# A factorization-machine tower on one core: the order of ScalarE's and VectorE's one-hot units in the first two chunks

## The chip, the core and the metric

One of the eight cores of a Trainium2 chip runs the whole program. The metric is the device time of one execution in microseconds (us), from which a median of several runs is taken. Engines are named TensorE (PE in the profile, its weight loads PEld), VectorE (DVE), ScalarE (ACT), GpSimd (POOL) and SyncE (SP, which only issues DMAs here).

## What is computed

For each of 2048 rows the kernel looks up 40 embeddings of 32 numbers, forms the 780 pairwise bilinear products and puts them, with 16 dense values, through a small MLP:

```
e = stack([tbl_f[ids[:, f]] for f in range(40)], axis=1)      # 2048 x 40 x 32
z = einsum('bke,kef,bkf->bk', e[:, I], W, e[:, J])            # 780 pairs (I < J)
h = concatenate([z, dense_ctx], axis=1)                       # 2048 x 796
h = maximum(h @ W_top1 + b_top1, 0)                           # 512
h = maximum(h @ W_top2 + b_top2, 0)                           # 256
y = h @ W_top3                                                # 1
```

## The kernel before

The batch is worked through in 4 chunks of 512 rows. The 40 fields stand in 10 groups of four; one group, transposed, fills a tile eT of 128 partitions (4 fields of 32) by 512. The pairs are put into 50 quads per chunk (`plan_quads`), numbered 0 to 199 over all chunks. For each quad TensorE does a `transform` (line 670, matmuls of line 680: weights times eT into the banks tps, in two halves), VectorE multiplies each half with another eT tile (line 660, into prods, which has three slots), and TensorE does a `reduce` (lines 692 to 705, into the bank zps). The rows of z of eight quads fill one tile; then ScalarE's `drain_z` (line 500) copies zps to zs, and the next `reduce` with slot 0 waits for it.

**How groups get into eT.** Sixteen fields have tables of 1000 rows: groups 0 to 3, the hot ones. Groups 4 to 9 are gathered by GpSimd (line 484) and transposed by VectorE (line 612), one quad before they are first needed. A hot group is looked up by matmuls: the table lies in SBUF in eight units of 128 rows, and for each unit u of a hot group h a one-hot tile `hot` of 128 x 2048 is made, which TensorE multiplies with three bf16 parts of the table (`look_up`, line 715, matmuls of line 733), 12 matmuls for a unit. All eight units of a group add up in the bank mlp_ps, and ScalarE's `drain_hot` (line 536, activation of line 540) copies it to eT. The next group's first look-up waits for that drain (`bank_free`). In the text (h, u) is unit u of hot group h; h runs over all chunks: 0 to 3 belong to chunk 0, 4 to 7 to chunk 1, and so on.

**Who makes a unit.** `by_scalar` (line 188) says it. VectorE makes one with a single comparison (line 605). ScalarE needs two activations (lines 531 and 534: absolute distance, then a relu). The tile `hot` has four slots, so unit number n waits until TensorE has used unit n - 4 (`hot_used`). The ids come by a DMA per group into one of three slots (`load_ids`, line 403).

**When.** `SIDES` says in which quad TensorE looks a unit up: groups 2 and 3 in quads 0 to 3, four units a quad; the 32 units of groups 4 to 7 from quad 7 on, in three of four quads. `MAKES` says in which quad's place in the queues a unit is made; for groups 4 to 7 that is two quads ahead on ScalarE and three on VectorE (line 213). VectorE makes the units of a quad behind that quad's two products (lines 662 to 664). `IDS_AT` places the loads of ids among SP's other issues, two quads behind the last unit that used the slot; `MIXED_AT` places the copies that build mixed tiles (`mix`, line 422), whose products are in the third and later quads after the pair's second group is first used.

Everything runs on TensorE in cycles (`CYCLES`): quad 0 alone, then two quads together. In a cycle TensorE does transform(at), reduce(at - 1), the look-ups of at, transform(at + 1), reduce(at), the look-ups of at + 1. ScalarE's queue for a cycle (lines 569 to 582) holds, in this order: the drains of MLP tiles, the z drain if a tile of eight quads ends, the drain of a hot group if its last unit is looked up in this cycle, and last the units to be made. Three units of groups 2 and 3 are written out ahead of the loop (lines 564, 566, 568), between the roundings of the table's parts (`round_part`); the matching remainders are VectorE's (`rest`, line 591), between its own first units (lines 625 to 640).

In chunks 1 to 3 the MLP of the chunk before (line 753) runs beside the quads; the last chunk's runs at the end.

Of the kernel before, what the change touches and what calls it, by code (L numbers as in the profile page):

```python
# [104 lines left out]
def mlp_out(layer, m):  # L105
    return sum(outs for _, outs in LAYERS[:layer]) + m
# [8 lines left out]
HOT_COUNT = (4, 4, 4, 4)  # L115
HOTS = [(t, g) for t in range(CHUNKS) for g in range(HOT_COUNT[t])]
GATHERED = [(t, g) for t in range(CHUNKS) for g in range(HOT_COUNT[t], GROUPS)]

UNITS, PARTS_OF = 8, 3
HOT_SLOTS = 4  # L120
# [67 lines left out]
def by_scalar(h, u):  # L188


    t, g = HOTS[h]
    return [g > 1 and u % 4 == 3, ((h - HOT_COUNT[0]) * UNITS + u) % 3 > 0, u % 2 == 1][min(t, 2)]


def made_until(h, u, scalar):

    return sum(by_scalar(h_, u_) == scalar for h_ in range(len(HOTS)) for u_ in range(UNITS) if (h_, u_) <= (h, u))
# [5 lines left out]
MAKES = {at: [] for at in range(TOTAL)}  # L203
MAKES[0] = [(2, u) for u in range(HOT_SLOTS, UNITS)]
for unit in range(UNITS):
    MAKES[1 + unit // HOT_SLOTS].append((3, unit))
for side_at, items in SIDES.items():
    for item in items:
        if item[0] == "hot" and HOTS[item[1]][0] > 1:
            MAKES[side_at - MADE_AHEAD].append(item[1:])  # L210
        elif item[0] == "hot" and HOTS[item[1]][0] == 1:

            MAKES[side_at - (2 if by_scalar(*item[1:]) else 3)].append(item[1:])


def steps_of(at):
    return [item for item in SIDES[at] if item[0] == "mlp"]
# [65 lines left out]
def wait(engine, semaphore, count):  # L283
    if count > 0:
        engine.wait_ge(semaphore, count)
# [11 lines left out]
def build(nc, ids, bases, table, hot_ids, hot_table, dense, wt, w1, b1, w2, b2, w3, out):  # L297
    ctx = ExitStack()
    with ctx:
# [77 lines left out]
        def slot_free(engine, k):  # L377

            if k >= ET_SLOTS:
                t, g = divmod(k - ET_SLOTS, GROUPS)  # L380
                engine.wait_ge(multiplied, 2 * (t * QUADS + last_quad(g) + 1))

        def slot_of(t, g):
            return (t * GROUPS + g) % ET_SLOTS
# [104 lines left out]
        @block.scalar  # L489
        def _(act):  # L490
            def split_at(g, part):

                return SPLITS.index((g, part)) + 1

            def drain_z(t, kt):
                if t == 0 and kt == 0:

                    act.wait_ge(remainder, len(SPLITS))
                act.wait_ge(reduced, t * QUADS + min((kt + 1) * PER_KT, QUADS))
                act.activation(zs[:, t % 2, kt, :], zps[:, :], ACT.Copy).then_inc(z_drained, 1)  # L500

            def drain_mlp(t, banks, layer, m):
                out_tile = mlp_out(layer, m)
                act.wait_ge(mlp_filled, t * MLP_OUTS + out_tile + 1)
                if layer < 2:
                    dst, bias = [(h1s, b1s), (h2s, b2s)][layer]
                    act.activation(dst[:, m, :], banks[out_tile], ACT.Relu,  # L507
                                   bias=bias[:, m:m + 1]).then_inc(mlp_drained, 1)
                else:
                    wait(act, y_stored, t * 16)  # L510

                    act.activation(y_s[:, :], banks[out_tile][:, 0:CHUNK // Q],
                                   ACT.Copy).then_inc(mlp_drained, 1)
                    act.wait_ge(mlp_drained, t * MLP_OUTS + MLP_OUTS)
                    act.dma_start(out[0:1, t * CHUNK:(t + 1) * CHUNK].rearrange("o (q b) -> (o q) b", q=Q),
                                  y_s[0:PART:EMB, :]).then_inc(y_stored, 16)

            def round_part(g, part):
                if part == 0:
                    act.wait_ge(hot_table_loaded[g], 16)  # L520
                else:
                    act.wait_ge(remainder, split_at(g, part - 1))
                act.activation(part_of[g][part], raw_parts[g], ACT.Copy).then_inc(rounded, 1)  # L523

            def make_unit(h, u):

                if u == [by_scalar(h, u_) for u_ in range(UNITS)].index(True):
                    act.wait_ge(hot_ids_loaded[h % IDS_SLOTS], 16 * (h // IDS_SLOTS + 1))
                act.wait_ge(hot_used, h * UNITS + u - HOT_SLOTS + 1)
                columns = hot[:, (h * UNITS + u) % HOT_SLOTS].rearrange("p q c -> p (q c)")  # L530
                act.activation(columns, ids16[:, h % IDS_SLOTS].rearrange("p q c -> p (q c)"), ACT.Abs,  # L531
                               bias=minus_code[:, u:u + 1]).then_inc(distances, 1)
                act.wait_ge(distances, made_until(h, u, True))
                act.activation(columns, columns, ACT.Relu, scale=-1.0, bias=ones[:, 0:1]).then_inc(hot_made_act, 1)  # L534

            def drain_hot(h):
                t, g = HOTS[h]
                act.wait_ge(hot_used, (h + 1) * UNITS)
                slot_free(act, t * GROUPS + g)
                act.activation(eT[:, slot_of(t, g), :], mlp_ps[:, :], ACT.Copy).then_inc(hot_drained, 1)  # L540

            def drain_sums(at):

                if at >= 0 and (at % QUADS == QUADS - 1 or at % QUADS % PER_KT == PER_KT - 1):
                    drain_z(at // QUADS, at % QUADS // PER_KT)

            def drain_tiles(steps):
                for _, t, layer, m, k in steps:
                    if k == LAYERS[layer][0] - 1:
                        drain_mlp(t, between_banks, layer, m)  # L550

            round_part(0, 0)
            round_part(0, 1)
            act.wait_ge(code_built, 1)
            act.activation(minus_code[:, :], code[:, :], ACT.Copy, scale=-1.0).then_inc(codes_turned, 1)
            round_part(1, 0)
            round_part(1, 1)
            round_part(2, 0)
            drain_hot(0)
            drain_hot(1)  # L560
            round_part(2, 1)
            act.wait_ge(codes_turned, 1)
            act.wait_ge(consts_built, 2 + Q)
            make_unit(2, 3)
            round_part(3, 0)
            make_unit(2, 7)
            round_part(3, 1)
            make_unit(3, 3)
            for cycle in CYCLES:
                at = cycle[0]  # L570
                if at == QUADS + 1:
                    act.wait_ge(mlp_loaded, 16 * 5)
                drain_tiles(steps_of(at))
                drain_sums(at - 1)
                if len(cycle) == 2:
                    drain_sums(at)
                for kind, *step in [item for quad in cycle for item in SIDES[quad]]:
                    if kind == "hot" and step[1] == UNITS - 1:
                        drain_hot(step[0])
                for unit in [unit for quad in cycle for unit in MAKES[quad]]:  # L580
                    if by_scalar(*unit) and unit not in ((2, 3), (2, 7), (3, 3)):
                        make_unit(*unit)
            drain_z(CHUNKS - 1, KT - 1)
            for layer, (_, outs) in enumerate(LAYERS):
                for m in range(outs):
                    drain_mlp(CHUNKS - 1, last_banks, layer, m)
            act.wait_ge(y_stored, 16 * CHUNKS)

        @block.vector
        def _(dve):  # L590
            def rest(g, part):

                dve.wait_ge(rounded, SPLITS.index((g, part)) + 1)
                if part == 1:
                    dve.wait_ge(remainder, SPLITS.index((g, 0)) + 1)
                dst = raw_parts[g] if part == 0 else part_of[g][2]
                dve.tensor_tensor(dst, raw_parts[g], part_of[g][part], ALU.subtract).then_inc(remainder, 1)

            def make_unit(h, u):
                if h == 0 and u == 0:  # L600
                    dve.wait_ge(code_built, 1)
                if u == [by_scalar(h, u_) for u_ in range(UNITS)].index(False):
                    dve.wait_ge(hot_ids_loaded[h % IDS_SLOTS], 16 * (h // IDS_SLOTS + 1))
                wait(dve, hot_used, h * UNITS + u - HOT_SLOTS + 1)
                dve.tensor_scalar(hot[:, (h * UNITS + u) % HOT_SLOTS], ids16[:, h % IDS_SLOTS],  # L605
                                  code[:, u:u + 1], None, ALU.is_equal).then_inc(hot_made_dve, 1)
# [27 lines left out]
            for u in range(UNITS):  # L634
                make_unit(1, u)
            rest(2, 0)
            for u in range(HOT_SLOTS - 1):
                make_unit(2, u)
            rest(2, 1)
            rest(3, 0)  # L640
# [2 lines left out]
            for at in range(TOTAL):  # L643
                t, n = divmod(at, QUADS)
# [221 lines left out]
```

## Time and profile before

| | us |
|---|---|
| runs | 693.02, 693.56, 695.09; median 693.56 |
| profiled execution | 690.86 |
| its span, first to last instruction | 689.1 |
| mean granted TensorE clock | 0.993 |
| TensorE busy | 653.5 (95%) |
| VectorE busy | 537.8 (78%) |
| ScalarE busy | 277.2 (40%) |
| GpSimd busy | 374.5 (54%) |

"Busy" is the time in which an engine had an instruction in work; TensorE's matmuls are pipelined and their ends are modelled, so that a short wait can hide in a longer matmul. A releaser (`<-`) is the instruction whose end let another start; `[1.99 <-ACT hot L534]` behind a line means that the engine stood idle 1.99 us until ScalarE's write of `hot` in line 534. `x12` is the number of instructions merged into a line. The granted clock is 1.00 at 2.4 GHz and 0.50 at 1.2 GHz. The chain that ended last is followed backwards from the last instruction, at each step to what released it. A slice of the page is 17.2 us.

### The profile page before, as it was taken

How to read it: one execution, taken by the hardware profiler on the slowest of the kernel's cores; microseconds unless marked ns; L12 is line 12 of the kernel's file. 1: busy time of each engine (PE TensorE's matmuls, PEld its weight loads, DVE VectorE, ACT ScalarE, POOL GpSimd, SP SyncE). 2: the span in 40 equal slices, each digit the busy share in tenths (PEclk: the TensorE clock that was granted, in tenths of full speed). 3: DMA queues.
4: the chain of work that ended last, by engine and by line, in shares of the span. 5: the costliest groups of instructions: out<-in, count | busy, mean ns of one | idle time of the engine just before them, and what ended most of it. 6: DMA issues, size and time to landing. Idle time of an engine off the chain costs nothing.

```text
span 689.1 us, 11819 instructions
## 1 busy us (share of the span) xinstructions
PE 653.5 (95%) x5120; PEld 203.5 (30%) x5120; DVE 537.8 (78%) x515; ACT 277.2 (40%) x196; POOL 374.5 (54%) x391
## 2 busy tenths in 40 slices
PE   3779889888999999999999999999999999999998
PEld 1222223222233333233333323333332323223233
DVE  6776789889879898879768989797767878789910
ACT  3634855876636455647034545655210000100002
POOL 5774576666566566565556556565564666560000
PEclk9989999999999999999999999999999999999999
DMA  7392111203320303012311202001202201101000
GB/s 250 103 377 86 48 52 41 58 13 87 79 68 11 87 12 88 10 43 58 87 23 46 87 11 57 10 14 46 66 13 55 55 13 20 48 12 48 1 1 0
DMA packets 26707, 39.40 MB, mean 57 GB/s; under 512 B 9168, under 2 KB 15456, under 8 KB 26528
## 3 DMA queue, kind: packets, MB, share of 16 engines
q1 hardware_dynamic: 14336, 32.33, 14.5%
q0 software_dynamic: 12288, 6.32, 6.1%
q8 instruction: 40, 0.66, 0.4%
q14 instruction: 11, 0.09, 0.0%
q10 hardware_dynamic: 32, 0.01, 0.0%
HBM read 22.88 MB, written 0.01 MB: 33 GB/s over the span
## 4 chain that ended last, share of the span: by engine, by line
PE 89%; ACT 5%; DMA 2%; DVE 2%; SPq 1%; issue 1%; DVEq 0%; ACTq 0%
PE tps L680 31%; PE zps L702 27%; PE mlp_ps L753 15%; PE mlp_ps L733 12%; PE tps L753 4%; ACT hot L534 2%; ACT hot L531 2%; DVE prods L660 2%; DMA eT<-eT 1%; DMA ids<-in_hot_ids 1%; SPq L432 1%; PE zps L689 0%; ACT zs L500 0%; ACT eT L540 0%; PE mlp_ps L758 0%
## 5 line engine op out<-in xcount | busy, mean ns | idle before, releaser
L660 DVE TENSOR_TENSOR prods<-tps,eT 128x1024 f32<-128x1024 f32 x400 | 468.6, 1217 | 109.9 <-PE tps L680 106.4
L484 POOL DMA_INDIRECT rows<-in_table,idx x384 | 373.8, 974 | 245.9 <-DVE prods L660 136.9
L680 PE MATMUL tps<-eT,weights 32*128 32x512 f32 x1600 | 242.9, 643 | 8.3 <-ACT eT L540 6.2
L702 PE MATMUL zps<-prods,select 128*32 128x512 f32 x1600 | 207.4, 607 | 0.8 <-DVE prods L660 0.3
L531 ACT ACTIVATE hot<-ids,minus_code 128x2048 bf16<-128x2048 int16 x57 | 113.7, 1994 | 41.1 <-PE mlp_ps L733 41.0
L733 PE MATMUL mlp_ps<-hot,parts 128*32 128x512 bf16 x1536 | 106.0, 390 | 23.6 <-ACT hot L534 10.8
L534 ACT ACTIVATE hot<-hot,ones 128x2048 bf16<-128x2048 bf16 x57 | 114.1, 2002 | 1.9
L680 PEld LDWEIGHTS tps<-eT,weights 32*128 32x128 f32 x1600 | 70.7, 183 | 135.9 <-DVE prods L660 72.1
L753 PE MATMUL mlp_ps<-zs,w1s 128*128 128x512 f32 x182 | 85.6, 608 | 0.0
L702 PEld LDWEIGHTS zps<-prods,select 128*32 128x32 f32 x1600 | 35.5, 108 | 150.7 <-DVE prods L660 88.5
L500 ACT ACTIVATE zs<-zps 128x512 f32<-128x512 f32 x28 | 16.7, 597 | 150.7 <-PE zps L702 144.5
L733 PEld LDWEIGHTS mlp_ps<-hot,parts 128*32 128x32 bf16 x1536 | 43.9, 99 | 110.3 <-issue 61.6
L605 DVE TENSOR_SCALAR hot<-ids,code 128x2048 bf16<-128x2048 int16 x71 | 52.1, 756 | 0.5 <-DMA ids<-in_hot_ids 0.4
L507 ACT ACTIVATE h1s<-mlp_ps,b1s 128x512 f32<-128x512 f32 x13 | 8.9, 687 | 101.4 <-PE mlp_ps L753 101.4
L753 PEld LDWEIGHTS mlp_ps<-zs,w1s 128*128 128x128 f32 x182 | 32.4, 189 | 51.2 <-issue 45.9
L540 ACT ACTIVATE eT<-mlp_ps 128x512 f32<-128x512 f32 x16 | 9.5, 596 | 53.2 <-PE mlp_ps L733 53.1
L753 PE MATMUL mlp_ps<-h1s,w2s 128*128 128x512 f32 x48 | 22.7, 610 | 0.0
L507 ACT ACTIVATE h2s<-mlp_ps,b2s 128x512 f32<-128x512 f32 x6 | 4.1, 687 | 41.5 <-PE mlp_ps L753 41.5
L753 PE MATMUL tps<-zs,w1s 128*128 128x512 f32 x42 | 18.6, 594 | 0.0
L612 DVE STREAM_TRANSPOSE eT<-rows 128x512 f32<-128x512 f32 x24 | 16.8, 702 | 0.0
L753 PEld LDWEIGHTS mlp_ps<-h1s,w2s 128*128 128x128 f32 x48 | 8.5, 189 | 13.7 <-issue 12.2
L523 ACT ACTIVATE parts<-zs 128x1024 bf16<-128x1024 f32 x8 | 8.3, 1050 | 9.8 <-DMA zs<-in_hot_table 4.9
(28 smaller groups left out, 44.6 us busy)
## 6 DMA issues: line engine op xcount, KB each, us to landing
ids<-in_hot_ids SPq DMA_DIRECT2D x16, 512.0 KB, 4.9
eT<-eT SPq DMA_DIRECT2D x40, 192.0 KB
rows<-in_table,idx POOLq DMA_INDIRECT x384
eT<-eT SPq DMA_DIRECT2D x40, 128.0 KB
eT<-eT SPq DMA_DIRECT2D x40, 64.0 KB
zs<-in_hot_table SPq DMA_DIRECT2D x4, 512.0 KB, 8.5
w1s<-in_w SPq DMA_DIRECT2D x1, 1792.0 KB
weights<-in_wt SPq DMA_DIRECT2D x1, 960.0 KB, 8.9
```

What stands on the lines that cost most here:

```text
L484: pool.indirect_dma_start(rows[:, k % ROW_SLOTS, m * EMB:(m + 1) * EMB], None, table, bass.IndirectOffsetOnAxis(ap=idx[:, g, t, m:m + 1], ...
L500: act.activation(zs[:, t % 2, kt, :], zps[:, :], ACT.Copy).then_inc(z_drained, 1)
L507: act.activation(dst[:, m, :], banks[out_tile], ACT.Relu, bias=bias[:, m:m + 1]).then_inc(mlp_drained, 1)
L531: act.activation(columns, ids16[:, h % IDS_SLOTS].rearrange("p q c -> p (q c)"), ACT.Abs, bias=minus_code[:, u:u + 1]).then_inc(distances, 1)
L534: act.activation(columns, columns, ACT.Relu, scale=-1.0, bias=ones[:, 0:1]).then_inc(hot_made_act, 1)
L605: dve.tensor_scalar(hot[:, (h * UNITS + u) % HOT_SLOTS], ids16[:, h % IDS_SLOTS], code[:, u:u + 1], None, ALU.is_equal).then_inc(hot_made_ ...
L612: dve.transpose(eT[:, slot_of(t, g), :], rows[:, k % ROW_SLOTS, :]).then_inc(transposed, 1)
L660: dve.tensor_tensor(prods[:, at % PROD_SLOTS, 2 * half:2 * half + 2, :], tps[:, (2 * at + half) % PAIR_BANKS, :, :], tiles, ALU.mult).then ...
L680: last = pe.matmul(tps[:, (2 * at + half) % PAIR_BANKS, bank, :], weights[part, n, :], eT[part, slot_of(t, g), :], start=True, stop=True)
L702: last = pe.matmul(zps[EMB * r:EMB * (r + 1), :], select[:, off:off + EMB], prods[:, at % PROD_SLOTS, bank, :], start=kt < KT - 1 and slot ...
L733: last = pe.matmul(mlp_ps[EMB * q:EMB * (q + 1), :], part_of[g][part][:, col:col + EMB], hot[:, at % HOT_SLOTS, q, :], start=u == 0 and pa ...
L753: last = pe.matmul(banks[out_tile], [w1s, w2s][layer][:, k, m * PART:(m + 1) * PART], [zs[:, t % 2, k, :], h1s[:, k % M1, :]][layer], star ...
```

## The change

It gives one unit of group 2 and one of group 3 to ScalarE, (2,5) and (3,5), instead of two each. (2,5) stands between the rounding of parts (3,0) and (3,1), (3,5) in the loop at the cycle of quads 3 and 4; VectorE makes the others, four of group 2 ahead of the loop instead of three. In ScalarE's loop the units of groups 2 to 7 (made for chunks 0 and 1) stand ahead of the cycle's drains; those of later chunks stay behind them. VectorE's units of groups 4 to 7 are made four quads ahead of their use instead of three. Two loads of ids follow in SP's order: that of group 6 from quad 4 to 5, that of group 8 from quad 26 to 25.

```
-    return [g > 1 and u % 4 == 3, ((h - HOT_COUNT[0]) * UNITS + u) % 3 > 0, u % 2 == 1][min(t, 2)]
+    return [g > 1 and u == 5, ((h - HOT_COUNT[0]) * UNITS + u) % 3 > 0, u % 2 == 1][min(t, 2)]
...
 for unit in range(UNITS):
-    MAKES[1 + unit // HOT_SLOTS].append((3, unit))
+    MAKES[3 if by_scalar(3, unit) else 1 + unit // HOT_SLOTS].append((3, unit))
...
-            MAKES[side_at - (2 if by_scalar(*item[1:]) else 3)].append(item[1:])
+            MAKES[side_at - (2 if by_scalar(*item[1:]) else 4)].append(item[1:])
...
             act.wait_ge(consts_built, 2 + Q)
-            make_unit(2, 3)
             round_part(3, 0)
-            make_unit(2, 7)
+            make_unit(2, 5)
             round_part(3, 1)
-            make_unit(3, 3)
             for cycle in CYCLES:
...
+                units = [unit for quad in cycle for unit in MAKES[quad] if by_scalar(*unit) and unit != (2, 5)]
+                for unit in units:
+                    if HOTS[unit[0]][0] < 2:
+                        make_unit(*unit)
                 drain_tiles(steps_of(at))
                 drain_sums(at - 1)
...
-                for unit in [unit for quad in cycle for unit in MAKES[quad]]:
-                    if by_scalar(*unit) and unit not in ((2, 3), (2, 7), (3, 3)):
+                for unit in units:
+                    if HOTS[unit[0]][0] > 1:
                         make_unit(*unit)
...
             rest(2, 0)
-            for u in range(HOT_SLOTS - 1):
+            for u in range(HOT_SLOTS):
                 make_unit(2, u)
             rest(2, 1)
```

## Rows read from the trace of the kernel before

**Rows 1.** The page: busy time and share by engine, then slices of TensorE and its clock.

```profile
PE 653.5 (95%) x5120; PEld 203.5 (30%) x5120; DVE 537.8 (78%) x515; ACT 277.2 (40%) x196; POOL 374.5 (54%) x391
...
PE   3779889888999999999999999999999999999998
...
PEclk9989999999999999999999999999999999999999
```

**Rows 2.** Waits, 66 to 200 us: engine, line <- releaser: us, times, longest.

```profile
PE mlp_ps L733 <- ACT hot L534: 10.4, 5, 2.6
```

**Rows 3.** TensorE in order of time, 66 to 205 us: start, us, operation, idle before.

```profile
75.71 0.90 PE L733 MATMUL mlp_ps<-hot,parts 128*32 128x512 bf16 x12 [1.99 <-ACT hot L534]
...
101.09 0.83 PE L733 MATMUL mlp_ps<-hot,parts 128*32 128x512 bf16 x12 [2.65 <-ACT hot L534]
...
114.66 1.50 PE L680 MATMUL tps<-eT,weights 32*128 32x512 f32 x8
...
124.73 0.83 PE L733 MATMUL mlp_ps<-hot,parts 128*32 128x512 bf16 x12 [1.93 <-ACT hot L534]
...
198.07 3.70 PE L753 MATMUL mlp_ps<-zs,w1s 128*128 128x512 f32 x8
```

**Rows 4.** ScalarE in order of time, 120 to 131 us.

```profile
120.16 0.60 ACT L500 ACTIVATE zs<-zps 128x512 f32<-128x512 f32 x1 [7.43 <-PE zps L702]
120.65 1.99 ACT L531 ACTIVATE hot<-ids,minus_code 128x2048 bf16<-128x2048 int16 x1
...
124.59 1.99 ACT L531 ACTIVATE hot<-ids,minus_code 128x2048 bf16<-128x2048 int16 x1
...
130.91 0.60 ACT L540 ACTIVATE eT<-mlp_ps 128x512 f32<-128x512 f32 x1 [2.30 <-PE mlp_ps L733]
```

**Rows 5.** TensorE in order of time, 36 to 57 us.

```profile
36.28 4.02 PE L733 MATMUL mlp_ps<-hot,parts 128*32 128x512 bf16 x48
44.98 1.51 PE L680 MATMUL tps<-eT,weights 32*128 32x512 f32 x8 [4.68 <-ACT eT L540]
...
48.12 3.22 PE L733 MATMUL mlp_ps<-hot,parts 128*32 128x512 bf16 x48
51.27 1.14 PE L680 MATMUL tps<-eT,weights 32*128 32x512 f32 x8
...
53.22 3.09 PE L733 MATMUL mlp_ps<-hot,parts 128*32 128x512 bf16 x48
```

**Rows 6.** ScalarE in order of time, 40 to 57 us.

```profile
40.40 2.00 ACT L531 ACTIVATE hot<-ids,minus_code 128x2048 bf16<-128x2048 int16 x1 [4.55 <-PE mlp_ps L733]
...
44.34 0.58 ACT L540 ACTIVATE eT<-mlp_ps 128x512 f32<-128x512 f32 x1
...
56.37 0.60 ACT L540 ACTIVATE eT<-mlp_ps 128x512 f32<-128x512 f32 x1 [0.94 <-PE mlp_ps L733]
```

**Rows 7.** VectorE in order of time, 60 to 117 us.

```profile
60.54 0.75 DVE L605 TENSOR_SCALAR hot<-ids,code 128x2048 bf16<-128x2048 int16 x1
...
64.68 2.36 DVE L660 TENSOR_TENSOR prods<-tps,eT 128x1024 f32<-128x1024 f32 x2 [1.12 <-DMA eT<-eT]
...
111.26 4.85 DVE L660 TENSOR_TENSOR prods<-tps,eT 128x1024 f32<-128x1024 f32 x4
116.03 0.70 DVE L612 STREAM_TRANSPOSE eT<-rows 128x512 f32<-128x512 f32 x1
```

**Rows 8.** TensorE in stretches: length, busy (matmuls), granted clock, DMA share, GB/s.

```profile
46.00:48.00 2.00, 2.00 (x12) 0.50 0.96 389
78.00:80.00 2.00, 2.00 (x12) 0.56 0.11 16
98.00:100.00 2.00, 0.45 (x7) 1.00 0.06 11
```

**Rows 9.** The chain that ended last, 55 to 66 us: start, us, what.

```profile
60.20 4.46 DMA eT<-eT
```

**Rows 10.** GpSimd in order of time, 104 to 109 us.

```profile
104.77 0.95 POOL L484 DMA_INDIRECT rows<-in_table,idx  x1 [0.30 <-issue]
```

## The prediction

> **What bounds the kernel now.** I read the page first: TensorE is busy 653.5 us of the 689.1 us span, and the slices of its line show where it isn't: almost all digits below 9 lie in the first eleven of 40 slices, that is in the start and in chunk 0; from chunk 1 on TensorE is full [rows 1]. The change touches only what is made for chunks 0 and 1, all of it made while chunk 0 runs. So a microsecond that TensorE saves before 198 us comes off the end whole, and nothing can be gained later.
>
> Next, the waits of 66 to 200 us: TensorE stood five times, 10.4 us together, for a unit that ScalarE had not finished [rows 2]. TensorE's own order of time shows the five: 1.99 us before the matmuls at 75.71, 2.65 before 101.09, 1.93 before 124.73, and twice more 1.93 (at 148.39 and 171.97) [rows 3]; added up 10.43. They come every eight quads, which is the rhythm of the z drains. ScalarE's order of time shows why: at 120.16 it drains z after 7.43 us of idling, only then starts the unit at 120.65, and needs two activations for it (until the next unit starts at 124.59: 3.94 us a unit); the stalled matmuls start at 124.73 [rows 3, 4]. The unit didn't depend on the drain; it stood behind it in ScalarE's queue. The five are (4,2), (5,0), (5,6), (6,4) and (7,2), used in quads 9, 17, 25, 33 and 41.
>
> At the start the same happens the other way round. Unit (3,3) waits until group 2 has been used up, starts at 40.40, and the drain of group 2 (eT at 44.34) stands behind it, although its bank was full at 36.28 + 4.02 = 40.30. TensorE stands idle 4.68 us, until 44.98 [rows 5, 6].
>
> **Part 1: group 2's and 3's units.** ScalarE gives up (2,3), (2,7), (3,3), (3,7) and takes (2,5), (3,5). VectorE gets two units more, at 0.75 us each [rows 7].
> - (2,3) is now a fourth VectorE unit ahead of rest(2,1). That delays the third part of group 2's first look-up by 0.75 us; the cover is the wait for the first mixed tiles, which ends with the same DMA as before, with over 1 us to spare. Cost nothing; if the cover is gone, 0.75 us.
> - (3,3) no longer stands ahead of drain_hot(2): the drain starts at 40.4 and transform(2) at 44.98 - 3.93 = 41.05. VectorE makes (3,3) behind the products of quad 1, before TensorE's look-ups of quad 2. **Gain 3.9**; the lower bound is 3.9 - 0.75, if VectorE's fourth unit is in the way.
> - The clock. In 46 to 48 us TensorE was granted 0.50, its level of 1.2 GHz, behind the gap of 4.68 us [rows 5, 8]. The stretch from transform(2) to transform(3) took 51.27 - 44.98 = 6.29 us; the same work of quad 3 took from 51.27 to 53.22 + 3.09 = 56.31, 5.04 us, at full clock [rows 5]. Without the gap I take full clock: **gain 1.2**. Bounds: 0 (the level falls all the same) and 1.25.
> - Look-ups of quad 3: (3,5) needs (3,1) used, which is so in the middle of quad 2's look-ups; it then has a transform and a reduce as cover. (3,6), (3,7) go to VectorE behind the products of quad 2, 1.5 us. drain_hot(3), before at 56.37 [rows 6], comes 5.1 us earlier; nothing more.
> - Mixed tiles of pair 1: SP issues them on drain_hot(3); the last copy took 4.46 us from 60.20 and VectorE waited 1.12 us for it [rows 7, 9]. The load of group 6's ids, which SP issued just ahead of these copies, now stands behind them (its quad goes from 4 to 5), so the copies don't share the DMA engines with 512 KB. And unit (4,0), 0.75 us between products of quads 4 and 5, is made while VectorE waits for transform(4). Together up to 1.12 + 0.75 = 1.87; (4,3), now ahead of quad 8's products, takes back some 0.3. **Gain 1.5**, bounds 0 and 1.87.
>
> **Part 2: units ahead of the drains.** (4,2) can start right behind (4,1), as its slot is long free; the others have the idle time ahead of the z drain: 7.43 us before 120.16 for 3.94 us of work [rows 4]. Each of the five stalls goes. **Gain 1.99 + 2.65 + 3 x 1.93 = 10.4.** With the first of them goes a half-speed stretch: granted clock 0.56 in 78 to 80 us, right behind the stall that ended at 75.71 [rows 3, 8]. **Gain 1.1**, sized like the other one. Bounds 0 and 1.25.
>
> What is late next? A unit that is still being made when a drain falls due. The narrowest place is between the z drain of 120.16 and the drain of group 5 at 130.91: 10.75 us apart now, 8.8 without the stall of 1.93. In it ScalarE has the z drain (0.49, from 120.16 to 120.65), (6,0) and now (6,1) too: 0.49 + 2 x 3.94 = 8.4 [rows 3, 4]. It fits with 0.4 us to spare, and behind it TensorE has a transform and a reduce, some 2 us, before it needs the bank. At drain 6 and at the z drains more is left. Cost nothing; without that cover up to 3.9 each.
>
> **Part 3: VectorE's units one quad sooner.** The same instructions, moved by one quad. They leave the place where TensorE runs a quad without look-ups, and enter the one ahead of it. Nothing was waiting for these units, but a product behind one is 0.75 later and those two quads on are no later. Cost and gain between -0.3 and +0.4 in each of nine four-quad stretches; I take 0.
>
> Does VectorE carry the faster pace? Four products take 116.03 - 111.26 = 4.77 us, so 1.19 each [rows 7]. From 75.71 to 198.07 [rows 3] lie 41 quads: 82 x 1.19 = 97.6, 10 units 7.5, five transposes 3.5: 108.6 of 122.4 us. Without the later four stalls (8.44) 114 are left, 5 more than VectorE needs. GpSimd: group 7's last gather was issued at 104.77, its transpose began at 116.03 [rows 7, 10]; with the stalls gone that lead loses 2 to 3 us of 11.
>
> **Sum.** 3.9 + 1.2 + 1.5 + 10.4 + 1.1 = 18.1 us. The profiled execution took 690.86 us (span 689.1), so it would come to 672.8. It was 2.7 us below the median of the three runs, 693.56; against that median I forecast **675.4 us**.
>
> **A rule for the other side.** ScalarE's drain of group 2 stood 3.93 us behind a unit it had nothing to do with [rows 6]. The Trainium skill, page "TensorE: Matmul & The Clock Gate", section "Architectural detail: the array is 16× 32×32, not 1× 128×128", says that ScalarE and VectorE take their queues strictly in order, only TensorE may reorder. By that rule a unit put ahead of a drain is as able to hold TensorE up as a drain ahead of a unit; the trace agrees in both directions.
>
> **Clock, rule and row.** The stall that ended at 101.09 is longer than that at 75.71, yet the clock stayed at 1.00 in 98 to 100 [rows 3, 8]. So the first slow stretch need not be the work of the stall. The same page, section "What's actually happening", says that the throttled state is the default and that activity lifts it. By it the fuller TensorE should keep 2.4 GHz, with the sum as it stands; by the row at 98 to 100 alone, 2.3 us of the sum would be open.
>
> **Rivals.**
> - *The slow stretches stay or move.* For it: the row at 98 to 100. Against: both stood right behind a gap. 18.1 - 2.3 = 15.8 gained, **677.7 us**. Chance 0.14.
> - *VectorE becomes the bound.* With 5 us of slack over 41 quads and products buffered only three deep, TensorE waits in small pieces where it stood in large ones. If half of the 8.44 comes back: **679.6 us**. For it: VectorE is on the chain already between the stalls. Against: it waits for TensorE in each stretch. Chance 0.15.
> - *More than forecast.* Behind each quad without look-ups a transform takes 1.50 us, as at 114.66, instead of 1.14 as at 51.27 [rows 3, 5]: it waits for products. Nine such places; if the earlier units remove them all, 3.2 to 3.6 more, **671.8 us**. Chance 0.07.
> - *Slower: drains held by units.* Eight drains in chunk 0 get a unit directly ahead of them (z0 to z4, groups 3, 5, 6). Each could be late by 3.94 less some 1.3 us that TensorE has in hand: 8 x 2.6 = 21.1, against 18.1 gained: 3 us slower, **696.6 us**. It decides from 2.3 us on at each drain, that is where a unit starts under 0.4 us before its drain falls due. Against it: the idle time of 7.43 ahead of the z drain [rows 4]. Chance 0.02.
> - *The order changes nothing*: the units wait for hot slots that come free only at the drains, and the stalls stay. Then only part 1 acts: 6.6 gained, **687.0 us**. Against: (5,6) needs (5,2), used five quads earlier. Chance 0.03; in 0.02 of it the gap at 40 to 45 is refilled by VectorE's units as well, and no difference is left that can be measured.
>
> The forecast keeps 0.59. The range 671.5 to 681.0 takes in the first three rivals and the bounds of the terms. A measurement of this kernel can tell about 0.3%, 2.1 us, from no change. Faster by more: 0.96, all cases but two; within: 0.02, the end of the last one; slower by more: 0.02, the drains held.
>
> **What would show it.** TensorE's waits for ScalarE's units between 60 and 200 us nearly gone; transform(2) at about 41; no gap of over 4 us at 40 to 45; granted clock 1.00 at 46 to 48 and around 70; the z drains behind two activations of a unit, at about 64, 86, 108, 130 and 151; the first MLP matmuls at about 180 instead of 198.07, and the same distance from there to the end. It is wrong if TensorE waits for eT or zs behind a unit, if VectorE has no waits left in chunk 0, or if the MLP start moves by less than 12.

## The result, and the profile after

The changed kernel takes 674.61 us, median of 4 runs (673.34 to 675.00), against 693.29 for the kernel before in 4 runs (691.10 to 695.09). The ratio is 0.9729 with a 95% interval from 0.9697 to 0.9760: 2.7% faster. The forecast was 675.4. The profiled execution took 673.34 us with a span of 671.5, so 17.6 us of span are gone, where the working had 18.1. Of the runs below, ten fell on chips where the kernel before itself took 814 to 848 us, with TensorE pausing where no other engine held it; those are set only against the kernel before as it ran beside them, and read for who waited for whom.

The page of the changed kernel: TensorE has lost 4 us of busy time, which goes with fewer stretches at the lower clock and shorter matmuls that no longer hold a wait, and the digits below 9 have gone from its slices behind the start [rows 1].

```profile
span 671.5 us, 11817 instructions
...
PE 649.5 (97%) x5120; PEld 204.6 (30%) x5120; DVE 538.2 (80%) x517; ACT 269.7 (40%) x192; POOL 373.3 (56%) x391
...
PE   3789999999999999999999999999999999999998
...
PEclk9989999999999999999999999999999999999999
```

The waits from 60 to 200 us. TensorE's own five waits for ScalarE's units, 10.4 us [rows 2], have no row any more; what is left is 0.6 us in its weight loads. VectorE still waits 12.2 us for TensorE, in 21 pieces.

```profile
DVE prods L665 <- PE tps L685: 12.2, 21, 1.9
...
PEld mlp_ps L738 <- ACT hot L535: 0.6, 2, 0.3
```

TensorE in order of time. transform(2), at 44.98 before, starts at 41.49; transform(3), at 51.27, at 46.14 [rows 5]; transform(4) at 51.95. The look-up of quad 9, which stood at 75.71 behind the first stall, starts at 67.30, and the first MLP matmuls at 180.55 instead of 198.07 [rows 3]. From there to the end it is 491.0 us in both traces (689.1 - 198.07 and 671.5 - 180.55): what was won in chunk 0 comes off the end whole.

```profile
41.49 1.14 PE L685 MATMUL tps<-eT,weights 32*128 32x512 f32 x8 [0.70 <-ACT eT L541]
...
46.14 1.14 PE L685 MATMUL tps<-eT,weights 32*128 32x512 f32 x8
...
51.95 1.14 PE L685 MATMUL tps<-eT,weights 32*128 32x512 f32 x8 [0.70 <-ACT eT L541]
...
67.30 0.86 PE L738 MATMUL mlp_ps<-hot,parts 128*32 128x512 bf16 x12
...
72.56 0.83 PE L738 MATMUL mlp_ps<-hot,parts 128*32 128x512 bf16 x12
...
180.55 3.70 PE L758 MATMUL mlp_ps<-zs,w1s 128*128 128x512 f32 x8
```

ScalarE drains group 2 at 40.84 and group 3 at 51.30, where it stood at 44.34 and 56.37 [rows 6]. The z drain at 108.12 (120.16 before) has no unit behind it that TensorE is waiting for, and group 5's drain follows at 117.05 after 0.48 us of idling [rows 4].

```profile
40.84 0.60 ACT L541 ACTIVATE eT<-mlp_ps 128x512 f32<-128x512 f32 x1 [6.09 <-PE mlp_ps L738]
...
51.30 0.60 ACT L541 ACTIVATE eT<-mlp_ps 128x512 f32<-128x512 f32 x1 [2.23 <-PE mlp_ps L738]
...
108.12 0.60 ACT L501 ACTIVATE zs<-zps 128x512 f32<-128x512 f32 x1 [4.59 <-PE zps L707]
...
112.55 1.99 ACT L532 ACTIVATE hot<-ids,minus_code 128x2048 bf16<-128x2048 int16 x1
...
117.05 0.60 ACT L541 ACTIVATE eT<-mlp_ps 128x512 f32<-128x512 f32 x1 [0.48 <-PE mlp_ps L738]
```

The granted clock is 1.00 where it was 0.50 and 0.56 [rows 8]. One stretch at the lower level stays, behind TensorE's wait for quad 0's first product (2.44 us, ending at 34.44), where it was before too (0.50 at 36 to 38 us in both traces):

```profile
36.00:38.00 2.00, 2.00 (x16) 0.50 1.01 404
...
46.00:48.00 2.00, 2.00 (x20) 1.00 0.95 344
...
78.00:80.00 2.00, 2.00 (x28) 1.00 0.79 238
```

### The profile page after: what moved, and what is told of

It reads as the page before. It is cut to its first block, busy times and chain, and to the rows that moved or that the text cites. A ratio compares the mean times of both kernels' runs of the same rounds, so it can differ in the third digit from the quotient of the medians.

```text
span 671.5 us, 11817 instructions
## 1 busy us (share of the span) xinstructions
PE 649.5 (97%) x5120; PEld 204.6 (30%) x5120; DVE 538.2 (80%) x517; ACT 269.7 (40%) x192; POOL 373.3 (56%) x391
## 4 chain that ended last, share of the span: by engine, by line
PE 94%; DVE 2%; DMA 1%; ACT 1%; SPq 1%; issue 0%; DVEq 0%; ACTq 0%
PE tps L685 33%; PE zps L707 29%; PE mlp_ps L758 16%; PE mlp_ps L738 12%; PE tps L758 4%; DVE prods L665 1%; DMA zs<-in_hot_table 1%; DMA eT<-eT 1%; SPq L433 0%; PE zps L694 0%; ACT eT L541 0%; ACT hot L532 0%; ACT hot L535 0%; PE mlp_ps L763 0%; DVEq L300 0%
## 5 line engine op out<-in xcount | busy, mean ns | idle before, releaser
L532 ACT ACTIVATE hot<-ids,minus_code 128x2048 bf16<-128x2048 int16 x55 | 109.7, 1995 | 37.8 <-PE mlp_ps L738 37.7
L535 ACT ACTIVATE hot<-hot,ones 128x2048 bf16<-128x2048 bf16 x55 | 110.1, 2002 | 1.8
L758 PEld LDWEIGHTS mlp_ps<-h1s,w2s 128*128 128x128 f32 x48 | 8.5, 189 | 13.7 <-issue 12.2
```

The source lines that it names most:

```text
L758: last = pe.matmul(banks[out_tile], [w1s, w2s][layer][:, k, m * PART:(m + 1) * PART], [zs[:, t % 2, k, :], h1s[:, k % M1, :]][layer], star ...
```

## The experiments

Twelve runs of five kernels. held_b and ahead_only_d, beside a kernel before of 689.03 and 691.70 us, settle most. Each of them is one execution, so their times carry no interval; it is their traces that are read.

### Part 1 alone (start_only, start_only_b, start_only_c)

```
-            MAKES[side_at - (2 if by_scalar(*item[1:]) else 4)].append(item[1:])
+            MAKES[side_at - (2 if by_scalar(*item[1:]) else 3)].append(item[1:])
...
-                    if HOTS[unit[0]][0] < 2:
+                    if HOTS[unit[0]][0] < 1:
...
-                    if HOTS[unit[0]][0] > 1:
+                    if HOTS[unit[0]][0] > 0:
```

> Part 1 alone: the new owners of the units of groups 2 and 3; units of groups 4 to 7 stand behind the drains and VectorE's are three quads ahead, as before. My theory (parts add up): the gap at 40 to 45 us and the half-speed stretch behind it go, TensorE's five waits for ScalarE's units stay, 10.4 us together; 5 to 7 us less than the kernel before, 687 to 688. Rival 'part 1 is worth nothing by itself': within 2 us of before. Rival 'the stalls go with part 1 too, because ScalarE has fewer units': under 5 us of waits and 676 to 680.

> The kernel of start_only again, on a chip where the kernel before takes its usual 691 to 695 us. Expected as there: the gap at 40 to 45 us gone, five waits of 10.4 us together still there, 687 to 688 us; the rivals as there (within 2 us of before; or the waits under 5 us and 676 to 680).

> The kernel of start_only once more, part 1 alone. Parts add up: five waits of 10.4 us together still there, 5 to 7 us less than the kernel before. Rivals: within 2 us of before; or the waits under 5 us and 13 us or more gained.

Ratios to the kernel before: 0.996 (0.992 to 1.000) in the first, none with an interval in the second (816.01 against 819.85), 1.002 (0.997 to 1.007) in the third. The first interval reaches to 7 us gained, the third stops at 3, so the 5 to 7 us expected were not seen. The traces show why these chips can't price part 1: the gap ahead of transform(2) is still there, 4.43, 3.48 and 5.32 us in the three runs, but no engine ends it. Here it is in start_only_b:

```profile
47.90 2.09 PE L685 MATMUL tps<-eT,weights 32*128 32x512 f32 x8 [3.48 <-issue]
```

The expectation that the gap goes was thus missed here. Where TensorE doesn't pause of itself, part 1 stays without a run of its own. Two traces with it can be set against two without it: transform(2) starts at 41.49 in the changed kernel and at 40.88 in held_b, against 44.98 in the kernel before and 44.74 in ahead_only_d. The waits for units can be read on any chip, here of start_only, 60 to 240 us:

```profile
PE mlp_ps L738 <- ACT hot L535: 10.2, 6, 3.4
```

10.2 us; in the repeats 10.4 and 11.8. So the rival that fewer units of groups 2 and 3 on ScalarE would do away with the stalls is out; the next runs show that the order does.

### Part 2 alone (ahead_only, ahead_only_b, ahead_only_c, ahead_only_d)

The kernel before, with the units of groups 4 to 7 ahead of the cycle's drains, and nothing else:

```
+                units = [unit for quad in cycle for unit in MAKES[quad]
+                         if by_scalar(*unit) and unit not in ((2, 3), (2, 7), (3, 3))]
+                for unit in units:
+                    if HOTS[unit[0]][0] == 1:
+                        make_unit(*unit)
                 drain_tiles(steps_of(at))
...
+                for unit in units:
+                    if HOTS[unit[0]][0] != 1:
                         make_unit(*unit)
```

> Part 2 alone: the units of groups 4 to 7 ahead of the cycle's drains; owners and VectorE's lead as before. My theory: the gap of 4.7 us at 40 to 45 stays, the five waits go, and with the first of them the half-speed stretch at 76 to 80; 10.4 + 1.1 = 11.5 us less than before, about 682. Rival 'VectorE becomes the bound': the waits go but only 5 to 8 us are gained. Rival 'the slow stretch has another cause': granted clock near 0.5 somewhere in 70 to 85 all the same, 10.4 us gained.

> The kernel of ahead_only again, on a chip where the kernel before takes its usual 691 to 695 us. Expected as there: the gap of 4.7 us stays, the five waits go, about 682 us; rival 'VectorE becomes the bound': 5 to 8 us gained; rival on the clock: granted clock near 0.5 in 70 to 85 all the same, 10.4 gained.

> The kernel of ahead_only once more, part 2 alone. Parts add up: the gap of 4.7 us at 40 to 45 stays, the five waits go, 11.5 us less than the kernel before. Rivals: VectorE becomes the bound (5 to 8 us gained); the half-speed stretch in 70 to 85 stays (10.4 gained).

> Part 2 alone, as one look. Parts add up: the gap of 4.7 us at 40 to 45 us stays and with it the half-speed stretch behind it; no wait for ScalarE's units from 60 to 200 us; no half-speed stretch at 70 to 85; the first MLP matmuls start at 198.07 - 11.5 = 186.6 us, give or take 1. Rival 'VectorE becomes the bound': they start at 190 or later with the five waits gone. Rival on the clock: granted clock near 0.5 somewhere in 70 to 85 although the stall is gone, start at 187.7.

The first three: 0.987 (0.981 to 0.993), 0.985 (0.980 to 0.991) and 0.998 (0.993 to 1.002); no row of TensorE's matmuls waiting for a unit from 60 to 240 us in any of the three. The third says less than the expected 11.5 us, 6 at most: the waits went there too, but these chips' own pauses fill the trace, so its time isn't explained further. TensorE also waited now and then for a drain that came late, here in ahead_only:

```profile
PE zps L707 <- ACT zs L500: 3.7, 2, 2.6
```

The fourth, ahead_only_d, took 678.41 us against 691.70 of the kernel before beside it, 13.3 less; its span is 676.6. TensorE in order of time:

```profile
44.74 2.09 PE L685 MATMUL tps<-eT,weights 32*128 32x512 f32 x8 [4.67 <-ACT eT L540]
...
51.52 1.14 PE L685 MATMUL tps<-eT,weights 32*128 32x512 f32 x8
...
57.27 1.14 PE L685 MATMUL tps<-eT,weights 32*128 32x512 f32 x8 [0.70 <-ACT eT L540]
...
73.26 0.83 PE L738 MATMUL mlp_ps<-hot,parts 128*32 128x512 bf16 x12
...
78.48 0.83 PE L738 MATMUL mlp_ps<-hot,parts 128*32 128x512 bf16 x12
...
185.67 3.70 PE L758 MATMUL mlp_ps<-zs,w1s 128*128 128x512 f32 x8
```

The gap of 4.67 us ahead of transform(2) is there, as it was; no bracket follows from 57.27 to the MLP. That starts at 185.67, 12.4 us earlier than in the first trace of the kernel before, against 11.5 expected, inside the 1 us that was allowed, and far from the 190 at which VectorE would have been the bound. Parts 1 and 3 bring it another 5.1 forward, to 180.55, where 6.6 had been put; part 3 accounts for some 0.8 of the difference (below). The stretches of TensorE, with the granted clock in the third place:

```profile
46.00:48.00 2.00, 2.00 (x12) 0.50 0.92 372
76.00:78.00 2.00, 2.00 (x16) 1.00 0.10 16
78.00:80.00 2.00, 2.00 (x28) 1.00 0.22 49
```

With the stall gone, so is the slow stretch at 76 to 80, while that behind the gap of the start is still there. The rival on the clock is out for this stretch. Its price can be read too: from the look-up of quad 9 to that of quad 11 it is 78.48 - 73.26 = 5.22 us here and 72.56 - 67.30 = 5.26 in the changed kernel; the forecast had 1.1 for it.

### Part 3 undone (lead3, lead3_c)

```
-            MAKES[side_at - (2 if by_scalar(*item[1:]) else 4)].append(item[1:])
+            MAKES[side_at - (2 if by_scalar(*item[1:]) else 3)].append(item[1:])
```

> The changed kernel with VectorE's units of groups 4 to 7 three quads ahead of use again instead of four: part 3 undone. My theory put it at 0, apart from the 0.75 us of unit (4,0) between the products of quads 4 and 5: start of the first MLP matmuls within 0 to 1 us of the changed kernel's. Rival 'more than forecast': 2 to 4 us slower than the changed kernel, since each quad without look-ups waits 0.4 us again.

> The kernel of lead3 once more, part 3 undone. Mine: the first MLP matmuls start within 0 to 1 us of the changed kernel's 180.55. Rival 'more than forecast': 2 to 4 us later.

0.9875 (0.980 to 0.995) and 0.985 (0.976 to 0.995) of the kernel before; the changed kernel wasn't beside them. They don't rule out 2 to 4 us; they only show that parts 1 and 2 gain without part 3. The rival's reason can be looked up in the changed kernel itself: it wanted the 1.50 us transforms behind the quads without look-ups to become 1.14, and with the earlier units they still take 1.58 (113.71) and 1.51 (124.43). What can be said of part 3 comes from the traces of the changed kernel and of ahead_only_d, which run the same instructions behind quad 9 apart from it. From the first z drain after quad 15 to that after quad 47 the changed kernel needs 173.37 - 86.59 = 86.8 us, ahead_only_d 178.49 - 92.32 = 86.2. From the look-up of quad 9 to the MLP it is 180.55 - 67.30 = 113.25 against 185.67 - 73.26 = 112.41. So VectorE's units a quad sooner look 0.6 to 0.8 us dearer. Where: in the changed kernel a transpose and a unit now stand two products apart, and TensorE's reduce at 110.00 has to wait for the product behind the unit. VectorE, then TensorE, of the changed kernel:

```profile
103.99 0.70 DVE L617 STREAM_TRANSPOSE eT<-rows 128x512 f32<-128x512 f32 x1
104.62 2.31 DVE L665 TENSOR_TENSOR prods<-tps,eT 128x1024 f32<-128x1024 f32 x2
106.86 0.73 DVE L610 TENSOR_SCALAR hot<-ids,code 128x2048 bf16<-128x2048 int16 x1
107.50 4.65 DVE L665 TENSOR_TENSOR prods<-tps,eT 128x1024 f32<-128x1024 f32 x4
```

```profile
108.63 1.27 PE L685 MATMUL tps<-eT,weights 32*128 32x512 f32 x8
110.00 1.06 PE L707 MATMUL zps<-prods,select 128*32 128x512 f32 x8
...
118.89 0.83 PE L738 MATMUL mlp_ps<-hot,parts 128*32 128x512 bf16 x12
...
121.60 0.61 PE L738 MATMUL mlp_ps<-hot,parts 128*32 128x512 bf16 x8
```

The four products from 107.50 take 4.65 us, so the first two, quad 24's, end at about 109.8. In ahead_only_d the unit comes two products later:

```profile
110.00 0.70 DVE L617 STREAM_TRANSPOSE eT<-rows 128x512 f32<-128x512 f32 x1
110.63 4.75 DVE L665 TENSOR_TENSOR prods<-tps,eT 128x1024 f32<-128x1024 f32 x4
115.30 0.78 DVE L610 TENSOR_SCALAR hot<-ids,code 128x2048 bf16<-128x2048 int16 x1
```

held_b, which has the earlier units too, repeats the pattern. From a transform to its reduce it is 1.37 us instead of 1.07 at three places one z tile apart, in both: 108.63, 130.45 and 152.20 in the changed kernel, 107.70, 133.81 and 155.57 in held_b:

```profile
107.70 1.27 PE L687 MATMUL tps<-eT,weights 32*128 32x512 f32 x8
109.07 1.06 PE L709 MATMUL zps<-prods,select 128*32 128x512 f32 x8
```

ahead_only_d has no such place behind quad 9. Three times 0.30 is a little more than the 0.6 found between those z drains, so something small was won back beside it. These are three single traces; no run undid part 3 alone on a chip without the pauses.

### A unit ahead of a drain at the wrong time (held, held_b)

The slower side's mechanism, made to happen once: (6,3), which can start only when (5,7) has been used, is put ahead of the drain that (5,7) makes due.

```
-                units = [unit for quad in cycle for unit in MAKES[quad] if by_scalar(*unit) and unit != (2, 5)]
+                units = [unit for quad in cycle for unit in MAKES[quad] if by_scalar(*unit) and unit not in ((2, 5), (6, 3))]
+                if 27 in cycle:
+                    units.append((6, 3))
```

> The changed kernel with one more unit put ahead of a drain: (6,3) ahead of the drain of group 5, for which it becomes free to start just when the drain falls due. In-order theory: that drain comes 3.9 us later than in the changed kernel, TensorE waits for it, 3.9 + 0.6 less the 2 us of transform and reduce it has in hand: 2.5 us of wait for eT near 118 us, all of it at the end. Rival 'TensorE's slack or VectorE's backlog covers it': no wait for eT, the first MLP matmuls start within 0.5 us of the changed kernel's.

> The kernel of held again, as one look: (6,3) ahead of the drain of group 5. In-order theory: TensorE waits some 2.5 us for that drain near 118 us if the chip runs at the times of the first result, and longer where the cover is thinner; everything behind it comes later by as much. Rival: no wait for eT there, as in the changed kernel.

In held_b (676.68 us against 689.03 of before beside it; the changed kernel's profiled execution took 673.34) ScalarE makes the unit first and drains at 120.07, and TensorE waits. ScalarE, then TensorE, of held_b:

```profile
116.12 2.00 ACT L532 ACTIVATE hot<-ids,minus_code 128x2048 bf16<-128x2048 int16 x1 [0.48 <-PE mlp_ps L740]
118.16 2.00 ACT L535 ACTIVATE hot<-hot,ones 128x2048 bf16<-128x2048 bf16 x1
120.07 0.58 ACT L541 ACTIVATE eT<-mlp_ps 128x512 f32<-128x512 f32 x1
```

```profile
117.08 1.06 PE L709 MATMUL zps<-prods,select 128*32 128x512 f32 x8
120.70 1.47 PE L740 MATMUL mlp_ps<-hot,parts 128*32 128x512 bf16 x12 [2.55 <-ACT eT L541]
...
124.97 0.83 PE L740 MATMUL mlp_ps<-hot,parts 128*32 128x512 bf16 x12
```

2.55 us, where 2.5 was expected: 3.95 of unit and 0.6 of drain, less what TensorE had in hand. ScalarE's queue is in order in this direction too. There is more: the matmuls at 120.70 take 1.47 us for twelve instead of 0.83, and the next look-up follows 4.27 us later (124.97 - 120.70), in the changed kernel 2.71 (121.60 - 118.89). The clock fell behind the gap:

```profile
120.00:122.00 2.00, 1.30 (x12) 0.64 0.12 16
122.00:124.00 2.00, 2.00 (x12) 0.50 0.05 8
124.00:126.00 2.00, 2.00 (x28) 1.00 0.08 16
```

So one late drain cost 2.55 + 1.56 = 4.1 us, over a third of it through the clock. The MLP starts at 183.92, 3.4 us later than in the changed kernel, although this run reached the look-up of quad 9 at 66.37, 0.9 us sooner: 4.3 us lost in between. In held (0.985 of before, 0.980 to 0.990) TensorE waited 10.2 us for drains of hot groups, 8.6 of it in one piece, against 0.5 in lead3, though held's 821.16 us aren't clear of lead3's 818.91; why one piece is so long stays open:

```profile
PE mlp_ps L740 <- ACT eT L541: 10.2, 2, 8.6
```

### The copies of the first mixed tiles (loads_later)

The changed kernel's quad 0 products started at 33.16, before at 32.54, and I took the weight loads beside the copies for the cause.

```
             mix(0, 0)
+            sp.wait_ge(mixed, 16 * 2 * len(MIXES))
             load_weights(1, 2)
...
-            for dst, src in ((w1s, w1), (w2s, w2), (w3s, w3), (b1s, b1), (b2s, b2)):
-                sp.dma_start(dst[:], src).then_inc(mlp_loaded, 16)
             load_dense(0)
             for at in range(TOTAL):
+                if at == 6:
+                    for dst, src in ((w1s, w1), (w2s, w2), (w3s, w3), (b1s, b1), (b2s, b2)):
+                        sp.dma_start(dst[:], src).then_inc(mlp_loaded, 16)
```

> The changed kernel, with SP waiting for the first six mixed copies to land before it issues the weights of quads 3 on, and with the MLP's weights issued at quad 6 instead of ahead of quad 0. In the changed kernel the last of these copies took 4.64 us beside four weight loads, and VectorE stood 3.48 us. Theory (the loads hold the copies up): the copies land 2 us after the last issue, VectorE starts quad 0's products near 30.9 instead of 33.16, and 2 us come off the end: about 2 us less than the changed kernel, that is 20 less than the kernel before. Rival 'the copies take 4 us by themselves': nothing gained, VectorE starts near 33, and quad 3 may wait for its weights.

819.64 us, 0.981 (0.973 to 0.989) of the kernel before, lead3_c beside it 824.36 (818.42 to 830.79), not clear of each other. SP's own order of time can be read all the same:

```profile
30.79 3.81 SPq L433 DMA_DIRECT2D eT<-eT  x6
37.72 0.34 SPq L421 DMA_DIRECT2D weights<-in_wt  x1
```

The last of six copies was issued at about 34.0 (30.79 + 3.81, less 0.6 for one issue), and SP, which waited for nothing but their landing, went on at 37.72: 3.7 us with no weight load beside them. With the loads beside them it was 4.00 before, 4.64 after, 3.84 in ahead_only_d, 4.13 in held_b, and 3.42 to 4.41 in four runs on the slower chips (held, start_only_c, start_only, lead3_c). The rival holds: the copies take nearly 4 us by themselves, and a cost of the loads isn't shown. My theory fell; why it was 4.64 in the changed kernel's trace stays open.

## Why the forecast was right, step by step

**The five stalls: right, and their cause shown.** 10.4 us were forecast, and with the clock 11.5 for part 2 alone; ahead_only_d gave 12.4 at the start of the MLP and 12.5 of span, against the kernel before's trace from another chip (13.3 against the execution beside it). The stalls stay when only part 1 acts and go when only the order changes.

**The start: the sum right by luck, its two terms off against each other.** I had 3.9 for the gap and 1.2 for the clock. transform(2) came 44.98 - 41.49 = 3.5 us earlier. The gap itself went as forecast, but quad 0's products had started 0.6 us later: I had taken the landing of the first mixed copies as fixed, and it isn't. VectorE's fourth unit was not in the way, as VectorE stood 3.48 us waiting for the copies. From the start of ScalarE's drain of group 1, which the copies wait for, to quad 0's products it is 8.1 us before, 8.7 after, 8.2 in held_b and 7.9 in ahead_only_d. And the stretch from transform(2) to transform(3) fell from 6.29 to 46.14 - 41.49 = 4.65 us, 1.6 less; the 5.04 that I had measured it by still held a wait for ScalarE's (3,7). Together 5.1, as forecast. The same wait is in the changed kernel: its quad 3 takes 51.25 - 46.14 = 5.11 us, and (3,5), made by ScalarE from 45.02 to 49.06, is on the chain that ended last. The cover that I had counted for it, a transform and a reduce, was some 0.5 us short (quad 2, with no such wait, took 4.65).

**The mixed copies of pair 1 and VectorE's units around them: right.** Group 3's drain came 56.37 - 51.30 = 5.1 us earlier, quad 6's products 64.68 - 58.16 = 6.5 [rows 6, 7], so 1.4 were won in between, where up to 1.87 had been put. All of it is the copies' landing, which ends VectorE's wait in both: from the last issue to the product it was 4.5 us before and is 3.0 now (issued at about 55.1), with the load of ids behind them. VectorE still waited for them, 0.36 us instead of 1.12:

```profile
58.16 2.36 DVE L665 TENSOR_TENSOR prods<-tps,eT 128x1024 f32<-128x1024 f32 x2 [0.36 <-DMA eT<-eT]
```

The look-up of quad 9 is 75.71 - 67.30 = 8.4 us earlier: 6.5, the first stall's 1.99, and 0.1 lost in between, where 0.3 was expected for (4,3).

**The slow stretch at 76 to 80: right.** 1.1 forecast, 1.1 to 1.15 measured (6.37 us from 75.71 to 82.08 before, 5.22 and 5.26 without it).

**The clock row that I set against it: misread.** The stretch 98 to 100 us lies inside the stall that ended at 101.09, not behind it. Behind the stall, from 102 to 106, the clock was 1.00 too, so the conclusion stands:

```profile
102.00:104.00 2.00, 2.00 (x18) 1.00 0.08 12
```

The three later stalls have no slow stretch behind them either, so the 1.1 us were the price of the first one alone.

**Part 3 at nothing: mis-sized, small.** The cost was in the bounds of the step, 0.3 a stretch, and I took 0; the traces put it at 0.6 to 0.8 us in all. From quad 9 to the MLP the kernel gained 122.36 (198.07 - 75.71) less 113.25, that is 9.1 us, where 9.5 had been put; without part 3, in ahead_only_d, it was 9.9. So the stalls and the slow stretch were worth 0.4 more than put and made up half of part 3's cost; the rest of the way from 18.1 to 17.6, 0.2 us, lies ahead of quad 9.

**What is late next: right.** The narrowest place was to have 0.4 us to spare, within 8.8 us. It has 0.48, and 117.05 - 108.12 = 8.93 us; in ahead_only_d it was 0.18. held_b shows what lies behind that edge. On the slower chips TensorE did wait for z drains, 1.8 to 4.6 us in the runs with units ahead of them, but also 0.9 to 2.9 in the three of start_only, which has none ahead. That the new order is free only at an even pace is therefore likely and not shown.

**Queue order and clock.** The Trainium skill's page "TensorE: Matmul & The Clock Gate" (section "Architectural detail: the array is 16× 32×32, not 1× 128×128") has ScalarE take its queue strictly in order; held_b agrees with 2.55 us. Its statement that activity lifts the throttle (section "What's actually happening") agrees with held_b, where the clock was 0.50 at 122 to 124 us and back at 1.00 from 124 on, after TensorE had been at work since 120.70. Why the stall that ended at 101.09 had no slow stretch behind it [rows 3] no run here settles.

## What to carry to other kernels

Look in the chain for work that stands in an in-order queue behind a wait it doesn't need: the price is its duration less what the waiting engine still has in hand (a unit of 3.94 us stalled TensorE by 1.93 to 2.65 here), each time, and moving it ahead costs nothing as long as its own inputs are ready early enough that it ends before the wait does. Compute that margin for the narrowest place and not only for the typical one; one drain 3.9 us late cost 2.55 us of wait here and 1.56 us of slow clock behind it. A wait that a later engine covers should be taken from the best and the worst landing seen, not from one trace.

## What I had not expected

The first six SBUF to SBUF copies of the mixed tiles take 3.4 to 4.6 us from the last issue to landing with weight loads beside them, and 3.7 in the one run without. Together with the 3.2 us in which one queue issues the five copies ahead of the last, they make up nearly all of the 8 us between the drain of group 1 and the first product. A gap that returns brings the slow stretch back at a place where there was none: granted clock 0.50 in 122 to 124 us of held_b.
